# A four-layer graph network on one core: the rank loop's x buffer in ten slots and pairs, and weight matrices split by quarters in layers 0 and 1

## The reference

```python
edge_index = jnp.stack([src, dst])
h = relu(layernorm(x)); x = x + L0(h, edge_index, W1, b1, W2, b2)      # two rounds of  relu(segment_sum((h @ W.T + b)[src], dst))
h = relu(layernorm(x)); x = x + L1(h, ...)   # layernorm(relu(((1+eps)*h + segment_sum(h[dst], src)) @ W1.T + b1) @ W2.T + b2) * gamma + beta
h = relu(layernorm(x)); x = x + L2(h, ...)   # mean of neighbours, own rows, relu, layernorm
h = relu(layernorm(x)); x = x + L3(h, ...)   # segment_sum(relu([h[src], h[dst]] @ W.T + b), src)
```

## Time and profile before

| | us |
|---|---|
| median of 3 runs | 2839.39 (2838.63 to 2842.8) |
| the profiled execution | 2838.36 |
| its span in the trace | 2836.3 |

### The profile page before, as it was taken

The page is one execution under the profiler, slowest core; times in us unless marked ns, Lnnn a source line. Parts: engine busy times, 40 slices in busy tenths (PEclk is TensorE's granted clock), DMA queues, the critical chain, the costliest instruction groups (busy, mean ns, idle before and its releaser), DMA issues. The chain is left out here.

```text
span 2836.3 us, 49619 instructions
## 1 busy us (share of the span) xinstructions
PE 2511.3 (89%) x13966; PEld 2147.9 (76%) x13966; DVE 2010.2 (71%) x5140; ACT 1351.2 (48%) x2794; POOL 1741.5 (61%) x1878
## 2 busy tenths in 40 slices
PE   4555269998899987999999969999999699999998
PEld 3444158887788877899999958888888588888886
DVE  7676656665566664788788768888888656666666
ACT  1655234444566655555555523333333245555554
POOL 0655435554677776777777647777777545555554
PEclk9999999999999998999999989999999899999999
DMA  8677533333455544433333334433333245555553
GB/s 252 190 217 210 173 136 96 109 117 99 137 152 165 174 154 125 124 116 113 113 113 113 102 94 125 132 114 113 114 114 114 83 139 152 153 154 156 150 151 116
DMA packets 146596, 387.99 MB, mean 137 GB/s; under 512 B 34423, under 2 KB 35383, under 8 KB 145882
## 3 DMA queue, kind: packets, MB, share of 16 engines
q0 software_dynamic: 101408, 304.38, 36.1%
q1 hardware_dynamic: 44010, 80.12, 9.0%
q10 hardware_dynamic: 1056, 2.10, 0.2%
HBM read 261.74 MB, written 149.28 MB: 145 GB/s over the span
## 5 line engine op out<-in xcount | busy, mean ns | idle before, releaser
L1582 PE MATMUL c_pu<-c_Zhi,parts 128*128 128x256 f32 x640 | 181.0, 283 | 10.2 <-DVE c_Zlo L1507 10.2
L1584 PE MATMUL c_pu<-c_Zhi,parts 128*128 128x256 f32 x640 | 182.6, 285 | 0.0
L1583 PE MATMUL c_pu<-c_Zlo,parts 128*128 128x256 f32 x640 | 182.2, 285 | 0.0
L838 POOL DMA_INDIRECT f_Gsrc<-rows,indexS x80 | 77.5, 969 | 168.9 <-PE f_phsrc L2078 163.7
L1996 ACT ACTIVATE f_Mhi<-f_pm 128x512 fp32r<-128x512 f32 x80 | 47.9, 599 | 266.6 <-DVE f_pm L2029 266.6
L2020 DVE TENSOR_TENSOR f_Hlosrc<-f_phsrc,f_Hhisrc 128x512 fp32r<-128x512 f32 x80 | 55.3, 692 | 167.6 <-ACT f_Hhisrc L1990 167.6
L1744 ACT CAST d_Hhi<-d_ph 128x512 fp32r<-128x512 f32 x80 | 46.8, 585 | 230.2 <-PE d_ph L1858 230.2
L842 POOL DMA_INDIRECT h<-a_rows,indexD x80 | 80.1, 1002 | 122.3 <-ACT a_rows L1159 118.1
L1474 ACT ACTIVATE c_pu<-c_pu,c_b1col 128x256 f32<-128x256 f32 x160 | 61.9, 452 | 161.5 <-PE c_pu L1584 161.5
L818 PE MATMUL a_po<-parts,a_Thi 128*128 128x512 f32 x320 | 132.2, 413 | 3.7 <-DVE a_Tlo L1194 3.6
L1582 PEld LDWEIGHTS c_pu<-c_Zhi,parts 128*128 128x128 f32 x640 | 122.1, 191 | 13.1 <-DVE c_Zlo L1507 11.5
(11 more groups left out here) (472 smaller groups left out, 9616.2 us busy)
## 6 DMA issues: line engine op xcount, KB each, us to landing
rows<-r_xt SPq DMA_DIRECT2D x20, 1040.0 KB, 6.4
h<-q_zerorow SPq DMA_DIRECT2D x80, 256.0 KB
r_xt<-in_x SPq DMA_DIRECT2D x80, 256.0 KB, 4.8
selrowsD<-selD SPq DMA_DIRECT2D x1, 2640.0 KB, 9.3
selrowsS<-selS SPq DMA_DIRECT2D x1, 2640.0 KB, 15.3
q_keyrowD<-in_dst POOLq DMA_DIRECT2D x1, 2560.0 KB
q_keyrowS<-in_src POOLq DMA_DIRECT2D x1, 2560.0 KB, 30.7
o_wstage<-in_L_W ACTq DMA_DIRECT2D x2, 1024.0 KB
```

What stands on the lines that cost most here:

```text
L838: return pool.indirect_dma_start(out, None, table, bass.IndirectOffsetOnAxis(ap=rows, axis=0))
L1582: pe.matmul(psum_u[:, o, :], g.Whi[2][:, c, cols], Zhi[:, c, :], start=c == 0, stop=False)
L1583: pe.matmul(psum_u[:, o, :], g.Whi[2][:, c, cols], Zlo[:, c, :], start=False, stop=False)
L1584: ins = pe.matmul(psum_u[:, o, :], g.Wlo[2][:, c, cols], Zhi[:, c, :], start=False, stop=c == C - 1)
```

## The change

Three things are edited.

1. `Tile.slot` and `Tile.use` count by the tile's own number where it is a plain integer, so that a ring need not divide the group.
2. The rank loop: `xt` has ten slots (RX). Statistics stay by tile; roots, scales and stores go by pairs. The scales of the pair (u-3, u-2) stand on VectorE ahead of odd tile u, ScalarE's root behind the tile after the pair. SyncE's order for each even u: store pair u, load tiles u+8 and u+9, one zero tile. `picked` for D lies in a tile that is no longer used. All five engines write out all their groups (`straight`), SyncE and VectorE in groups of ten.
3. In a_ and c_ a matrix is split in four parts: behind group i, ScalarE copies quarter c of matrix n, where n and c are quotient and remainder of i by 6, and GpSimd subtracts the quarter that ScalarE made behind the group before. For ScalarE the first ten groups are written out. Load and hand-over semaphores count in quarters. In layer 2 the matrices are split whole as before, and in the third block of `prepare_orders` too.

```diff
     def slot(self, ring):
-        return self.j % ring
+        return (self.t if isinstance(self.t, int) else self.j) % ring
...
-            picked = {k: f.sb("picked" + k, [P, P], F32) for k in KEYS}
+            picked = {"D": iota_i[:, :].bitcast(F32), "S": f.sb("pickedS", [P, P], F32)}
...
-            xt = f.sb("xt", [P, U, EXT], F32)
-            ln = RootNorm(f, "ln", QUAD, 2)
-            q_x, q_ext = f.sems("q_x", U), f.sems("q_ext", QUADS)
+            RX = 10
+            xt = f.sb("xt", [P, RX, EXT], F32)
+            ln = RootNorm(f, "ln", 2, 2)
+            q_x, q_ext = f.sems("q_x", RX), f.sems("q_ext", RX // 2)
...
                 def load(T):
-                    s, q = T.slot(U), T.slot(U) // QUAD
-                    wait(sp, q_ext[q], 16 * T.use(U))
-                    sp.sem_inc(q_tick, 1)
+                    s = T.slot(RX)
+                    wait(sp, q_ext[s // 2], 16 * T.use(RX))
                     sp.dma_start(xt[:, s, 0:D], io.x[bass.ds(T.t * P, P), :]).then_inc(q_x[s], 16)
...
-                    for u in range(0, U, QUAD):
-                        at(i, u + 1, -5, U, NT, store)
-                        for n in range(QUAD):
-                            at(i, u + 2, 2 + n, U, NT, load)
-                        for n in range(QUAD // 2):
-                            at(i, u // 2 + n, 0, U // 2, NT // 2, zero)
+                    for u in range(0, RX, 2):
+                        at(i, u, 0, RX, NT, store)
+                        for n in range(2):
+                            at(i, u + n, 8, RX, NT, load)
+                        at(i, u, 0, RX, NT, zero)
...
-                    for u in range(U):
-                        if u % QUAD == 1:
-                            at(i, u, -QUAD - 1, U, NT, scale_x)
+                    for u in range(RX):
+                        if u % 2:
+                            at(i, u, -3, RX, NT, scale_x)
...
-                pipeline(dve, GR, 1, 1, body)
+                straight(NT // RX, 1, 1, body)
...
-                        if u % QUAD == 0:
-                            at(i, u, -QUAD, U, NT, root_x)
+                        if u % 2 == 0:
+                            at(i, u, -2, U, NT, root_x)
...
+    def high_part(self, act, i):
+        n, c = divmod(i, C + 2)
+        if n < len(self.sources) and c < C:
+            slot = self.sources[n][0]
+            act.wait_ge(self.loaded, 16 * (n + 1))
+            self.nc.scalar.copy(self.g.Whi[slot][:, c, :], self.stage[:, c, :]).then_inc(self.high, 1)
+
+    def low_part(self, pool, i):
+        n, c = divmod(i - 1, C + 2)
+        if 0 <= n < len(self.sources) and c < C:
+            slot = self.sources[n][0]
+            pool.wait_ge(self.high, C * n + c + 1)
+            pool.tensor_tensor(self.g.Wlo[slot][:, c, :], self.stage[:, c, :],
+                               self.g.Whi[slot][:, c, :].bitcast(F32), ALU.subtract).then_inc(self.low, 1)
...
-                pipeline(act, GR, 1, 1, body, between=lambda n: W.split_high(act, n))
+                pipeline(act, GR, 1, 1, body, between=lambda i: W.high_part(act, i), first=2 * C + 2)
```

More of the change, by code:

```diff
@@ L59, in at, with pipeline @@
         stage(tile)
-def pipeline(eng, groups, lead, drain, body, ahead=2, between=None):
-    first, last = 2, groups - ahead
+def pipeline(eng, groups, lead, drain, body, ahead=2, between=None, first=2):
+    last = groups - ahead
     for i in range(-lead, first):
@@ L361, in _ @@
                 sp.wait_ge(q_const, 2 * R + 1)
-                pipeline(sp, GR, 1, 1, body)
-                for q in range(QUADS):
-                    sp.wait_ge(q_ext[q], 16 * GR)
+                straight(NT // RX, 1, 0, body)
+                for q in range(RX // 2):
+                    sp.wait_ge(q_ext[q], 16 * (NT // RX))
                 sp.wait_ge(q_zero, 16 * NT)
@@ L393, in statistics_x @@
                 def statistics_x(T):
[L394 to L395 removed]
+                    dve.wait_ge(q_x[T.slot(RX)], 16 * (T.use(RX) + 1))
+                    ln.statistics(dve, T, xt[:, T.slot(RX), 0:D])
                 def aggregate_x(T):
@@ L436, in _ @@
                 pool.wait_ge(q_const, 2 * R)
-                pipeline(pool, GR, 0, 1, body)
+                straight(GR, 0, 1, body)
                 for k in KEYS:
@@ L511, in body @@
                         at(i, u, 0, U, NT, look)
-                pipeline(pe, GR, 0, 0, body)
+                straight(GR, 0, 0, body)
         c12.close()
@@ L776, in load_one @@
     def load_one(self, sp, n):
-        wait(sp, self.low, n)
+        wait(sp, self.low, C * n)
         sp.dma_start(self.stage[:, :, :], self.sources[n][1].rearrange("(c p) n -> p c n", p=P))\
@@ L827, in straight @@
         body(i)
-        if between and 0 <= i < 2:
+        if between and 0 <= i:
             between(i)
@@ L908, in number @@
     def number(self, T):
-        each = T.unroll // self.group
-        return T.k * each + T.j // self.group
+        return T.use(self.group)
     def statistics(self, dve, T, rows):
@@ L1099, in _ @@
             pool.wait_ge(s_const, 4 if second else 3)
-            straight(NT // RING, 1, 1, body, between=W and (lambda n: W.split_low(pool, n)))
+            straight(NT // RING, 1, 1, body, between=W and (lambda i: W.low_part(pool, i)))
             for s in range(RING):
@@ L1442, in _ @@
             pool.wait_ge(s_const, 3 + U)
-            straight(GR, 2, 1, body, between=lambda n: W.split_low(pool, n))
+            straight(GR, 2, 1, body, between=lambda i: W.low_part(pool, i))
             for s in range(U):
@@ L1490, in _ @@
             act.wait_ge(s_prep, 1)
-            pipeline(act, GR, 2, 0, body, between=lambda n: W.split_high(act, n))
+            pipeline(act, GR, 2, 0, body, between=lambda i: W.high_part(act, i), first=2 * C + 2)
         @block.vector
@@ L1723, in _ @@
             pool.wait_ge(s_const, 2 + 2 * R)
-            straight(GR, 1, 1, body, between=lambda n: W.split_low(pool, n))
+            straight(GR, 1, 1, body, between=lambda n: n < 2 and W.split_low(pool, n))
             for s in range(R):
```

34 lines of the change are left out of this document (16 added, 18 removed).

## The result

The changed kernel takes 2796.8 us (median of 6 runs, 2795.63 to 2797.65), the kernel before, run beside it, 2840.8 us (median of 6, 2838.63 to 2842.8). The ratio is 0.9845, 95% interval 0.9835 to 0.9856. The forecast was 2797, within 2787 to 2814. One execution of a later kernel (the rank loop alone) took 2900.2 us at a mean granted clock of 0.896 instead of 0.98 and is left out; all other executions are compared as they are. The profiled execution of the changed kernel has a span of 2794.8 us, against 2836.3 before: 41.5 us less.

What follows compares the result with a forecast made beforehand. The prediction took VectorE's wait for x to bound the rank loop and TensorE's stops around weight splitting layers 0 and 1. 2838.4 - 32.5 (rank loop) - 3.9 (layer 0) - 4.9 (layer 1) = 2797.1 us; range 2787 to 2814.

Steps and rivals of the forecast that it cites:

- What bounds the kernel: Rank loop: no engine full, VectorE waits 40.6 us for x; layers 0 and 1: only what stops TensorE counts.
- the 31.9 us: Rank loop: tile 79 picked at 279.5 instead of 311.41, from 2.14 us per tile and 1.11 per set.
- The set of two columns at 1.11 us: VectorE, rank loop: two columns cost the same as four, so 20 more sets cost 22.2 us.
- Rival (c): Rank loop: cheaper two-column sets leave GpSimd's 2.53 us per tile as floor, 12.5 us more gain, about 2785; chance 0.10.
- The turn to the next stage: End of rank loop: next stage 8.9 us after the last pick instead of 10.1, gaining 1.2 us.
- The 0.6 us held back for the roots: Start of rank loop: ScalarE's first root comes two tiles earlier into a filling pipeline; 0.6 us deducted.
- Layer 0: Quarters hold VectorE at most 1.0 us, under 2.2 of slack; both TensorE stops go, gaining 3.9 us.
- Layer 1: Quarters keep c_ylen at 5.6 us at worst, under 5.9; both TensorE stops go, 5.2 us lost, 4.9 kept.
- What starts earlier: All stages start earlier, so granted-clock stretches may fall otherwise over layer starts, a few microseconds either way.
- (a): Rank loop: transfers set the pace at 6.3 us per pair, no gain there, about 2829, half-way 2820; chance 0.11.
- (b): Rank loop: every pair waits for its own store, 39 times 3.74 us, kernel near 2943; chance 0.04.
- (d): Layers 0 and 1: quarters don't help, gain 0, total 2806; chance 0.13, in full or in part.

Runs made afterwards that it cites:

- the rank loop alone: The changed kernel with the weight matrices of layers 0 and 1 split whole again; 2809.7 us, ratio 0.9867.
- written out alone: The kernel before with only the rank loop's five hardware loops written out, still eight slots and fours; 2842.1 us, ratio 0.9978.
- quarters alone: The kernel before with the split by quarters in layers 0 and 1 and its old rank loop; 2836.3 us, ratio 0.9956.
- first and third groups: Follow-up kernels, each group on one chip: first the parts one by one, third the disputed costs; kernel before 2848.8 and 2851.5 us.
- the second group: Follow-up kernels on one chip, varying the sizes of the pieces; the kernel before took 3018.3 us there.
- fours again: The changed kernel with roots and scale sets by fours, ten slots kept, loads ten tiles ahead; ratio 0.9912 on one chip, 2819.9 us (0.9891) on another.

## Why the prediction was right, point by point

- **What bounds the kernel.** Right. VectorE's wait for x went from 40.6 us to nothing, and VectorE is the pace. The sum from its own pieces met the last pick to 0.1 us (279.5 and 279.55). That is closer than its terms are: a set adds 1.06 us instead of 1.11, 1.9 us less over 38 sets, and tiles that take longer than 2.15 (2.53, 2.37, 2.26 and others) make up for it.
- **Where the 31.9 us come from.** The forecast took the whole difference at once, by the pace of written-out tiles. The runs take it apart. Keeping the loops costs 13.6 us in pairs. Of that 24 sets x 0.15 = 3.6 are for slower sets of scales, and the kernel before has only 12 sets in its loop, 1.8. So its loop cost 11.8. Then 40.6 (wait for x) + 11.8 (loop) - 21.2 (20 more sets at 1.06) = 31.2, against 31.9; 0.7 us stay without a name. The terms come from two chips. The word "pairs" thus names the larger part of the gain, but a good third of it is the missing hardware loop. This part can be had in full only once VectorE isn't waiting: written out alone, it brought 6.7 us.
- **The set of two columns at 1.11 us.** Right: in most pairs 3.21 - 2.15 = 1.06, and 18.2 us less work with 20 sets fewer. Rival (c), the larger gain, assumed otherwise and fell.
- **The turn to the next stage.** This term was mis-sized: 8.9 us after the last pick, measured 10.7. I let the turn follow GpSimd's last scatter for the most part, where SyncE's wait for the last store (4.9 us before, 4.8 after) ends just ahead of the next stage in both kernels. And I overlooked the zero tile that the new order puts behind that store. The change's list of instructions had it. With it taken ahead, the turn is 9.6 us, 1.1 to 1.9 shorter. The expected gain of 1.2 became a loss of 0.6, as the old turn took 10.1. The 0.6 us held back for the roots at the start were not needed, and so the error in the rank loop is 1.2 us in all.
- **Layer 0.** Right: 4.2 us for 3.9. The comparison is held 0.7 us (0.95 instead of 0.25), under the 1.0 allowed, and the quarter takes 1.31 where 1.28 was taken. That a VectorE instruction is held until GpSimd's ends is now shown at three sizes: 4.06 us beside the whole matrix (3.95 with only GpSimd's part whole), 1.77 beside halves, 0.95 beside quarters. In every one of the 16 subtractions of layer 0 in these four traces the comparison that started behind it ended 0.05 to 0.08 us after it; how long it was held is what was left of GpSimd's operation (4.59, 2.43, 1.31 us). The Trainium skill, "GPSIMD Engine Reference", section Key points, speaks only of contention on shared SBUF interfaces. Had it been a slowdown spread evenly over all work, quarters would have won nothing.
- **Layer 1.** The mechanism is right, the size was 4.9 and came out as 5.9. The 5.2 us that the two stops cost were cut to 4.9 for a margin of 0.3 us that was never used: c_ylen starts at worst 5.06 us into a pair, not 5.6. The sum began from 3.46 us, but in that pair c_ylen was still on its way back: undisturbed it starts at 2.94, and 2.94 + 1.28 + 3 x 0.3 is 5.1. From the third pair on the pairs are 13.93 to 14.0 us long throughout. Counted over 37 pairs the stops cost 5.3 us, and a pair without a stop takes 13.98 us instead of 13.99, some 0.4 in all; the last 0.2 have no row of their own.
- **What starts earlier.** The forecast left this open. The stretches of lower granted clock fall otherwise over the starts of the stages: after layer 0 to the gain's side (1.2 us; in the first 30 us of the next part the mean granted clock is 0.94 instead of 0.90), at the start of layer 1 against it. Here the stretch at the start of layer 1, from its first products (c_pu) to the first of its second products (c_po), before and then after:

```profile
1083.30:1105.60 22.30, 18.81 (x146) 18.54 (x146) 9.95 (x13) 14.04 (x24) 10.37 (x11) 0.92 0.27 73
```

```profile
1046.50:1070.30 23.80, 20.32 (x146) 20.08 (x146) 6.97 (x14) 14.02 (x24) 10.84 (x12) 0.86 0.27 76
```

  The same 146 matmuls take 1.5 us more at a mean granted clock of 0.86 than at 0.92. The two cancel to 0.1 us.
- **The rivals.** (a), the transfers as the pace, didn't come: 239 GB/s in the loop, and a load lands in 4.6 us. (b), a handshake for each pair, didn't come, but the run with fours shows how near it lies: there the loads wait again for stores just issued, and 37 us of waiting come back, 22 us in all. (d) is refuted by the run with the rank loop alone.
- **The sum.** The rank loop gave 1.2 less than the sum, layer 0 0.3 more, layer 1 1.0 more, the clock -0.1, which nearly cancel. The time was met to 0.3 us, while its single terms are good to about 1 us: the closeness is luck. So is the starting point: the sum begins from an execution of 2838.4 us, and the median of the kernel before, over six, is 2840.8. By medians the change won 44.0 us, where the sum has 41.3.

## What to carry to other kernels

When a ring of buffers is loaded, used and stored, what counts is whether the load about to be issued waits for the store *just* issued or for one a step older; count that distance in steps of the ring, not in slots: pairs in eight slots did all that ten did, and fours in ten, with loads into the slots just stored, lost 22 us. Written-out code is worth its full price only when the engine that is the pace isn't waiting for something else (12.4 us here once the wait for x was gone, 6.7 before). At the end of a stage list everything that the stage's last wait covers, helpers such as zero fills too, and put what depends on nothing ahead of what is late.

## What the runs showed of the hardware that was not expected

- The same rank loop of the kernel before ended at 321.5 us in one trace and at 331.6 in another (quarters alone), with 40.6 and 50.2 us of waiting for x in 18 turns. The medians don't explain it: loads land in 4.8 and 4.9 us, and SyncE waited no longer for the stores (106.8 and 104.5 us). Which transfer was late is not shown. The changed loop ended at 290.3, 290.6 and 290.8 in the first measurement and in the first and third groups.
- On the chip of the second group the changed loop took 42 us more, with pauses of some 2 us in about every fourth tile, and the second call of `layer0` some 145 us more, at a granted clock of 0.87. The cause of both is open.
- A short VectorE instruction (a comparison, 0.25 us) that started behind a GpSimd subtraction ended 0.05 to 0.08 us after it, each of 16 times, whether that lasted 4.6, 2.4 or 1.3 us.
- The last store was waited for 4.8 and 5.6 us in two traces with a 256 KB transfer issued right behind it, and 4.5 us in one without.
- A set of six short dependent instructions on VectorE took 0.15 us more inside the hardware loop than written out, and the rest of a tile 0.14 us more (2.29 us instead of 2.15); each of the six branches added about 0.5 us.
- Two stores of 520 KB issued together land in 8.5 us in the median (fours again); issued singly, in 4.4 (the changed kernel, first measurement).
